# A graph layer's dense steps: the output bias as a product of one row on TensorE, the blocks started two steps later, and their last two stages two steps sooner

## The reference, cut to what matters

```python
out = segment_sum(attn[:, None] * v[src], dst)      # attention over the edges
out = out @ Wo + bo
h = out + x
x = layernorm(x + (gamma * (h - mean(h)) / sqrt(var(h) + 1e-5) + beta))
h = _layer_norm(x, ln1_w)                           # opens the second layer
xl = h @ lin_l_w.T + lin_l_b                        # the two tables that the
xr = h @ lin_r_w.T + lin_r_b                        # second layer gathers from
```

## Time and profile before

| what | value |
|---|---|
| median of three runs | 2989.43 us (2985.38 to 2994.2) |
| the profiled execution, its own time | 2994.84 us |
| its span in the profile | 2993.0 us |
| mean granted TensorE clock | 0.826 of 2.4 GHz |
| dense steps of layer 0 (step 204 to the last table) | from 1320 to 1449 us of the span |

### The profile page before, as it was taken

One profiled execution on the slowest core, in us unless ns is written; L12 is line 12 of the kernel. 1 busy time (PEld: TensorE's weight loads), 2 busy tenths in 40 slices (PEclk: granted clock), 3 DMA queues, 4 the chain that ended last, 5 costly groups with the idle time before them and its releaser, 6 DMA issues. The chain is left out here.

```text
span 2993.0 us, 52671 instructions
## 1 busy us (share of the span) xinstructions
PE 2201.2 (74%) x14461; PEld 1756.5 (59%) x14461; DVE 1718.3 (57%) x7092; ACT 1126.6 (38%) x2973; POOL 1725.0 (58%) x1739
## 2 busy tenths in 40 slices
PE   7766665666666666667578888887888887888779
PEld 5665665665555666556355555555555665656556
DVE  2355555555555555557346656666666666666766
ACT  2355555555555555555333222222222222222123
POOL 3356666666666666655565656666666666666322
PEclk9687788788788877887788888987888888888879
DMA  5344444444444444432644444444444444444201
GB/s 136 97 117 111 109 112 105 113 113 109 109 111 114 106 112 112 123 88 59 171 148 141 147 142 126 144 143 140 144 146 147 144 131 139 146 146 147 62 20 36
DMA packets 378501, 356.41 MB, mean 119 GB/s; under 512 B 61695, under 2 KB 335743, under 8 KB 371424
## 3 DMA queue, kind: packets, MB, share of 16 engines
q1 hardware_dynamic: 314640, 236.51, 28.3%
q0 software_dynamic: 53248, 109.16, 14.2%
q10 hardware_dynamic: 10320, 7.37, 0.9%
HBM read 338.98 MB, written 13.82 MB: 118 GB/s over the span
## 5 line engine op out<-in xcount | busy, mean ns | idle before, releaser
L846 POOL DMA_INDIRECT rows<-xl_tab,src_cols x832 | 844.0, 1014 | 505.9 <-issue 228.1
L279 POOL DMA_INDIRECT rows<-in_x,src_cols x832 | 796.6, 957 | 537.0 <-issue 208.9
L330 PE MATMUL tile_sums<-gather,rows 128*128 128x128 f32 x1664 | 420.1, 342 | 254.4 <-DVE node_sums L560 172.4
L560 DVE TENSOR_TENSOR node_sums<-node_sums,tile_sums 128x256 f32 x832 | 350.0, 421 | 387.1 <-PE tile_sums L332 182.9
L330 PEld LDWEIGHTS tile_sums<-gather,rows 128*128 128x128 f32 x1664 | 322.9, 241 | 296.7 <-issue 190.1
L320 PE MATMUL p_dst<-window,spread 128*128 128x129 f32 x1664 | 331.1, 333 | 200.9 <-issue 154.1
L1022 DVE SCALAR_TENSOR_TENSOR node_sums<-node_sums,shrunk,tile_sums 128x128 f32 x832 | 280.7, 337 | 238.2 <-remote 175.6
L320 PEld LDWEIGHTS p_dst<-window,spread 128*128 128x128 f32 x1664 | 283.6, 241 | 219.8 <-issue 207.6
L332 PE MATMUL tile_sums<-gather,ones 128*128 128x128 f32 x1664 | 389.8, 323 | 0.0
L548 DVE CUSTOM_DVE_ANT_0 product<-rows,p_dst 128x128 f32<-128x128 f32 x832 | 258.2, 348 | 226.3 <-remote 147.7
L909 PEld LDWEIGHTS z_ps<-spread,window 128*128 128x128 f32 x1664 | 254.6, 221 | 155.2 <-issue 132.9
(11 more groups left out here) (187 smaller groups left out, 2525.7 us busy)
## 6 DMA issues: line engine op xcount, KB each, us to landing
window<-p_tab SPq DMA_DIRECT2D x832, 64.5 KB
attr<-in_attrT SPq DMA_DIRECT2D x52, 1024.0 KB
window<-xr_tab SPq DMA_DIRECT2D x832, 64.0 KB
rel_bc<-rel_rows SPq DMA_DIRECT2D x208, 128.0 KB
rel_bc<-rel_rows SPq DMA_DIRECT2D x52, 512.0 KB
rows<-in_x,src_cols POOLq DMA_INDIRECT x832
rows<-xl_tab,src_cols POOLq DMA_INDIRECT x832
p_tab<-p_rows ACTq DMA_DIRECT2D x13, 258.0 KB, 3.5
```

What stands on the lines that cost most here:

```text
L279: nc.gpsimd.indirect_dma_start(out=rows[:, r, i, :], out_offset=None, in_=t["x"], in_offset=bass.IndirectOffsetOnAxis(ap=src_cols[:, tile: ...
L330: nc.tensor.matmul(tile_sums[k][:, i, 0, :], rows[:, Q % AHEAD0, 2 * k + i, :], gather1[:, Q % 2, 2 * k + i, :], start=True, stop=True)
L560: nc.vector.tensor_tensor(span, span, tile_sums[i // 2][:, i % 2, :, :], ALU.add).then_inc(added, 1)
L846: nc.gpsimd.indirect_dma_start(out=rows[:, r, i, :], out_offset=None, in_=xl_tab, in_offset=bass.IndirectOffsetOnAxis(ap=src_cols[:, tile: ...
```

## The change

The bias moves to PE: after each of the four products with `w_vo`, a product of one row adds (denominator row of the node) x (`b_vo`) to `o_ps`. Divided by the denominator later, that is the bias. `bias_x`, `beta_o` and the semaphore `x_biased` go, and `residual` and POOL wait for the loaded rows themselves. The stages `moments1`, `root1`, `invert1`, `turn_y`, `keep_hT` come two steps sooner behind the projection (two or three instead of four or five), and `tables`, `keep_tables` four steps behind it instead of six. `DENSE` is 206, so block b is projected two steps later and its turn and tables stay in the steps they had. The number of steps stays 223. Since the first loads of `x_nm` are tied to `DENSE`, they come two steps later too.

```diff
-    DENSE = 204
+    DENSE = 206
-        beta_o = sb("beta_o", [P, P])
-        steps = max(quads + 2, DENSE + blocks + 6)
+        steps = max(quads + 2, DENSE + blocks + 4)
-                    pool.wait_ge(x_biased, b + 1)
-                    nc.gpsimd.tensor_tensor(x1[:, b, 0:n], x_nm[:, b % QT, 0:n], beta_o[:].unsqueeze(1).to_broadcast(wide),
+                    pool.wait_ge(x_nm_in[b % QT], (b // QT + 1) * DMA)
+                    nc.gpsimd.tensor_tensor(x1[:, b, 0:n], x_nm[:, b % QT, 0:n], beta[:].unsqueeze(1).to_broadcast(wide),
-                    if b >= 6:
-                        pe.wait_ge(hT_made, b - 5)
+                    if b >= 4:
+                        pe.wait_ge(hT_made, b - 3)
...
-                        mm = nc.tensor.matmul(o_ps[:, i, :], node_sums[:, 0, at:at + P], w_vo[:], start=True, stop=True)
+                        nc.tensor.matmul(o_ps[:, i, :], node_sums[:, 0, at:at + P], w_vo[:], start=True, stop=False)
+                        mm = nc.tensor.matmul(o_ps[:, i, :], node_sums[0:1, 1, at:at + P], b_vo[0:1, :], start=False,
+                                              stop=True)
...
-                    pe.wait_ge(inverted, min(b + 6, blocks))
+                    pe.wait_ge(inverted, min(b + 4, blocks))
...
-                    if 0 <= b - 5 < blocks:
-                        turn_y(b - 5)
-                    if b == 6:
+                    if 0 <= b - 3 < blocks:
+                        turn_y(b - 3)
+                    if b == 4:
                         pe.wait_ge(w_scaled, 2)
-                    if 0 <= b - 6 < blocks:
-                        tables(b - 6)
+                    if 0 <= b - 4 < blocks:
+                        tables(b - 4)
...
-                    dve.wait_ge(x_biased, b + 1)
+                    dve.wait_ge(x_nm_in[b % QT], (b // QT + 1) * DMA)
...
-                        nc.vector.tensor_tensor(beta_o[:], beta[:], b_vo[:], ALU.subtract)
-                    if 0 <= b + 1 < blocks:
-                        bias_x(b + 1)
-                    if 0 <= b - 5 < blocks:
-                        invert1(b - 5)
+                    if 0 <= b - 3 < blocks:
+                        invert1(b - 3)
-                    if 0 <= b - 4 < blocks:
-                        moments1(b - 4)
+                    if 0 <= b - 2 < blocks:
+                        moments1(b - 2)
```

More of the change, by code:

```diff
@@ L190, in build @@
         bv_spread = sem("bv_spread")
-        x_biased = sem("x_nm_biased")
         x_nm_in = [sem(f"x_nm_in{i}") for i in range(QT)]
@@ L515, in _ @@
                         root0(b - 1)
-                    if 0 <= b - 5 < blocks:
-                        root1(b - 5)
+                    if 0 <= b - 3 < blocks:
+                        root1(b - 3)
                     if T < quads:
@@ L521, in _ @@
                         norm0(b - 1)
[L522 to L525, removed]
+                    if 0 <= b - 3 < blocks:
+                        keep_hT(b - 3)
+                    if 0 <= b - 4 < blocks:
+                        keep_tables(b - 4)
             @block.vector
@@ L620, in invert1 @@
                     nc.vector.reciprocal(rstd[:, 1, b % 2, 0:n], std[:, 1, b % 2, 0:n]).then_inc(rstd1_made, 1)
[L622 to L626, removed]
                 nc.vector.memset(ones[:], 1.0)
```

## The result

The changed kernel takes 3026.01 us, median of four runs (3023.84 to 3035.4), against 2991.8 (2985.38 to 2994.2) for the kernel before, which now has four runs as well. The ratio is 1.0123, interval 1.01 to 1.0147. It is slower by 1.2%, outside the range of 2977 to 2997, and on the other side of the forecast 2986.7.

The account below looks back on a forecast made before the run. It took no engine as full in mixed steps, where the lists run in turn, and loops through ACT and POOL behind dense steps. Its terms summed to -2.7 us, from median 2989.43 to 2986.7 us, range 2977 to 2997.

Parts of the forecast that it names:

- term 3: Step 206, now the first mixed step: centring product 0.5 us plus bias rows 1.0, together +1.5 us.
- if PE never idles before its turn: Dense steps: one of the signs the prediction named that would show it wrong; it expected PE still idling there.
- rival C: Dense steps: PE becomes their bound, each wholly low-clock step costing about 4 us; three of eight give +9; chance 0.10.
- Rival B: Steps 207, 208 and 210: bias rows keep PE's clock high, -9.7 us more, total -12.4, 2977.0 us; chance 0.17.
- Terms 1 to 3: Steps 204 and 205 as attention alone -13.1 us, end of step 203 -0.4, step 206 +1.5.
- rival D: Step 204's odd 2.7 us wait for denominators returns in step 206: sum 0, 2989.4 us; chance 0.19.
- Term 5: Step 209: bias rows fill the projection's lead over DVE's moments; 0 us, bounds -0.6 and +0.6.
- Term 7: Dense steps 210 to 218: eight of 5.65 us plus 1.5 for short clock falls, 46.7 us, so +11.0.
- loop (a): Dense steps: DVE's shift ends with POOL's L290, then ACT's u and POOL's operations lead round again; 5.60 us a round.
- Term 8: Tail, steps 217 to 222 before: two steps fewer at 3.72 us each, -7.4 us.
- term 4: Steps 207 and 208 at the low clock: bias rows +1.9 us each, w_cen copy 0.35 in 207; +4.2 us.
- term 6: Step 210: PE has no room for the bias rows; +1.5 us, bounds +1.0 and +1.9.

Follow-up runs that it names:

- full-row kernel: The changed kernel with the bias product taking all 128 rows (denominators times b_vo / 128) instead of one: 2939.95 us, 0.9968 of the kernel before.
- schedule alone: The kernel before with only the change's DENSE 206 and shorter stage distances, the bias still on DVE: 2938.56 us, 0.9951 of the kernel before.

## Why the prediction was wrong

The step that failed is the price in term 3, used again in terms 4 to 7: "a one-row product of 129 columns takes 437 ns in the mean, the full one beside it 430. The row count saves nothing", and then 0.126 and 0.234 us a record. A mean length says how long a record lies in the pipeline. What it costs is the distance from its start to the next start, and that was there to read in the trace of the kernel before, where L308 and L309 alternate:

```profile
71.99 0.50 PE L308 MATMUL lr_ps<-m_aug,xT 128*128 128x129 f32 x2
72.42 0.48 PE L309 MATMUL lr_ps<-m_bias,ones 1*128 1x129 f32 x2
72.83 0.49 PE L308 MATMUL lr_ps<-m_aug,xT 128*128 128x129 f32 x2
```

0.42 us for two records, where equal neighbours take 0.22. I took the pitch from eight equal records and put the rows in between. In a block at the high clock, the projection takes 3.3 us (eight products at 0.415) instead of 1.0, and at the low one 5.8 (1379.16 to 1384.95 in the trace) instead of 1.9. The forecast added 1.0 and 1.9; the trace 2.3 and 3.9. For a record among its equals the 0.126 and 0.234 were about right: the traces have 0.11 and 0.22 from start to start.

With that price PE is the bound even at the high clock. As an estimate, denominators of 0.98 (1398.66 to 1399.64), the projection of 3.3, and 2.3 for turn and tables (1379.01 to 1381.30 in the full-row kernel) make 6.6 us for a dense step, not the 5.3 of the prediction. Over eight steps that is 6 us more than the 46.8 of the full-row kernel. The other 30 came with the lower clock. The prediction had named the sign: "if PE never idles before its turn".

The second failure is in the chance of rival C, 0.10. Its mechanism happened: PE became the bound, at a granted clock of 0.62 over the dense steps. It was said to need three of eight steps wholly at the low clock; all eight took about 10 us, each only partly at the low clock, because the bias rows cost more than this rival had counted too. Against it I set that "PE had less to do" in the high-clock steps, as if more records kept the clock up. The order with the bias rows first shows that these records don't: 0.75 granted at 100% busy, against 1.00 at 92% busy with full rows. Rival B, which hoped that the bias rows would keep the clock high, had it the wrong way round.

The Trainium skill says that the time of a weight load goes by columns, not by rows, and that a load of 32 rows takes as long as one of 128 (TensorE: Matmul & The Clock Gate, LDWEIGHTS). The traces agree for the load by itself, 187 ns in the median for the one-row bias when these products stand together, and 192 for the full ones of the full-row kernel. They add that a load with another row count than the product in front starts later, by about 0.2 us at the high clock and 0.3 at the low one.

What held, by its own steps:

- Terms 1 to 3: -10.7 against -12.0, or -13.0 without the bias rows of step 206, which come behind the mark. The two attention steps were 13.2 us from clip to clip instead of 10.5; single attention steps in this trace take from 3.5 to 9.8 us, so a mean over two of them was a weak figure. DVE's gap before the first reciprocal was 2.91 us with PE as releaser, against 5.84 before, so the prediction's rival D did not show.
- Term 5: +1.6 instead of 0, and +1.1 in the full-row kernel.
- Term 7's loops. With full rows the dense step is 5.62 us, and it is 5.61 without any bias, so PE's work does not set it. DVE is busy 36.7 of 46.8 us, and POOL's round in the trace (three operations of 1.26 to 1.28 us and a wait of 1.78 for ACT's `u`) fills the step. That fits loop (a); no run cut the loop. `bias_x` was worth 0.4 a step: with it, 6.06 in the schedule alone. From the reciprocal of 210 to the last block's the full-row kernel took 7.50 + 7 x 5.62 = 46.8 us, and the term said 46.7. Its 1.5 us for short falls of the clock stand against 1.9 more in the first step alone, which is near by luck.
- Term 8: -7.3 against -7.4.
- The shorter distances made no wait: in the full-row kernel DVE starts `moments1` with no idle time before it.

The full-row kernel is the change with the bias row at the price I gave it. It came to 0.9968, -10 us by medians, where the sum says -2.7. Against the trace of before (which is from another chip) its parts are -13.8 for terms 1 to 3, +2.5 for term 4 instead of +4.2, +1.1 for term 5, -0.5 for term 6 instead of +1.5, +11.1 for term 7 and -8.9 for term 8 instead of -7.4: -8.4 together, counted from the unrounded marks. Part of that is the clock in the mixed steps, which varies: in two profiles of one and the same kernel, from the reciprocal of 207 to that of 208 took 10.21 us at a granted clock of 0.83 and 12.74 at 0.63. How much of the rest is chance stays open.

## What to carry to other kernels

Take the cost of a PE record from start to start in the same neighbourhood of shapes, never from its mean length. Where a small product has to stand among full ones, either give it all the rows (its operand padded with zeros or divided by the row count), or put all products of one row count together. Full rows were the better of the two here in the profile (dense steps of 5.62 against 6.88 us). And look whether the kernel already does it wrong elsewhere, since that was worth 1.2% here against 0.5% for the schedule.

## What the runs showed of the hardware

- A change of the row count between neighbouring products costs about 0.2 us at 2.4 GHz and 0.3 at 1.2 GHz, from 128 to 1 and from 128 to 64 alike (a product of two records every 0.42 and 0.73 us instead of 0.22 and 0.43).
- Sixteen one-row records in a row, of 36 in a step, went with a falling clock: fully busy, PE was granted 0.75. With eight of them in full rows it was 1.00, at 92% busy. Eight one-row records or none made no difference (0.96 from step 210 to 218).
- Alternating row counts went with a low clock too, on a PE that was busy all the time: 0.62 for 128 and 1, 0.74 for 128 and 64.
- DVE's four-column `shift` (L602 in the kernel before) still ended with POOL's sum (L290) when `bias_x` was gone: 0.97 to 0.98 us in the full-row kernel, beside a POOL sum of 1.26, in a round of 5.62. In the kernel before the same operation took 0.16 us in the mixed step at 1336.86.
- The same kernel before took 2950 us in one group of runs and 2543 to 2552 in two others; only ratios carry over.
